# Keeping twelve instead of nine feed-forward blocks of an image for its successor's stage in a convolution-attention and feed-forward kernel

## The reference

```
x = x + conv(ln_over_channels(x))      # linear attention over 32 heads of dim 8
t = tokens(x)                          # 1024 tokens x 256
t = t + ffn(ln_over_channels(t))       # 6 experts of width 341, gated per image

conv: qkv = 1x1(x); agg = grouped 1x1(depthwise 5x5(qkv)); heads from [qkv, agg]
      kv = relu(k)^T [v, 1]; out = relu(q) kv; out = out[:8] / (out[8] + eps)
      then 1x1 projection and batch norm
ffn:  token_repr = mean over tokens; softmax over 11 router logits; top 2;
      expert weights from a fixed table; h = gelu(t W1 + b1);
      sum over experts of weight * (h W2 + b2)
```

## Time and profile before

| | |
|---|---|
| time, median of 3 runs | 1707.79 us (1707.75 to 1715.56) |
| the profiled execution: time | 1710.06 us |
| its span | 1708.3 us |
| PE busy (matmul) | 1370.4 us, 80% |
| DVE busy | 1281.9 us, 75% |
| ACT busy | 1059.6 us, 62% |
| POOL busy | 970.8 us, 57% |
| mean DMA rate | 19 GB/s |

### The profile page before, as it was taken

How to read it: one execution, slowest core, us unless ns; L and a number is a source line. 1 busy time by engine, 2 the same in 40 slices (tenths; PEclk the granted TensorE clock), 3 DMA queues, 4 the chain that set the end, 5 groups by cost and what they waited for, 6 DMA issues and landing times.

```text
span 1708.3 us, 18712 instructions
## 1 busy us (share of the span) xinstructions
PE 1370.4 (80%) x6844; PEld 786.2 (46%) x6844; DVE 1281.9 (75%) x1305; ACT 1059.6 (62%) x1855; POOL 970.8 (57%) x746
## 2 busy tenths in 40 slices
PE   5516557699878989699878989699878987999598
PEld 3215435455444545455444545355444444545343
DVE  3995999896959976896959966896959987880000
ACT  3444435577648765677648765677657865675376
POOL 3682726466558557465567556475565647344444
PEclk7758779899989999899989999899989999999899
DMA  5100000000001100100001100100001000100000
GB/s 174 74 25 1 25 1 1 0 26 13 1 0 38 37 1 1 38 25 13 1 1 38 38 1 1 38 1 13 1 1 37 13 1 1 37 13 1 13 1 25
DMA packets 14251, 32.75 MB, mean 19 GB/s; under 512 B 2384, under 2 KB 5328, under 8 KB 13904
## 3 DMA queue, kind: packets, MB, share of 16 engines
q1 hardware_dynamic: 14160, 31.56, 5.3%
HBM read 23.17 MB, written 8.39 MB: 18 GB/s over the span
## 4 chain that ended last, share of the span: by engine, by line
PE 48%; ACT 19%; POOL 13%; DVE 11%; issue 8%; DMA 1%; SPq 0%; POOLq 0%; ACTq 0%; DVEq 0%
PE wbk L542 20%; PE acc L555 12%; DVE dacc L1121 8%; PE wbk L634 7%; POOL dwo L939 4%; ACT gh L739 4%; ACT hb L740 3%; PE wbk L644 2%; PE wbk L593 2%; ACT tapb L714 2%; POOL tl L903 2%; POOL gl L969 2%; ACT sum_b L819 1%; ACT qkvs L790 1%; PE wbk L608 1%
## 5 line engine op out<-in xcount | busy, mean ns | idle before, releaser
L1121 DVE SCALAR_TENSOR_TENSOR dacc<-qkvs,dww,dacc 128x930 f32<-128x930 f32 (+4 forms) x954 | 1053.0, 1184 | 0.0
L969 POOL TENSOR_TENSOR gl<-hb,gh 128x512 f16<-128x512 f32 x256 | 303.5, 1187 | 385.3 <-ACT hb L740 384.6
L834 ACT ACTIVATE hb<-wbk,b1s 128x512 f32<-128x512 f32 x256 | 175.0, 684 | 201.2 <-PE wbk L542 201.0
L939 POOL TENSOR_TENSOR dwo<-dwo,tapb 128x992 f32<-128x992 f32 (+1 forms) x104 | 240.9, 2316 | 11.7 <-ACT tapb L714 8.4
L542 PE MATMUL wbk<-th,w1h 128*128 128x512 f16 x512 | 158.1, 391 | 104.7 <-POOL tl L903 65.4
L555 PE MATMUL acc<-gh,w2h 128*128 128x512 f16 x512 | 197.8, 386 | 13.6 <-POOL gl L969 13.5
L555 PE MATMUL acc<-gl,w2h 128*128 128x512 f16 x512 | 197.6, 386 | 0.0
L555 PE MATMUL acc<-gh,w2l 128*128 128x512 f16 x512 | 197.3, 385 | 0.0
L739 ACT ACTIVATE gh<-hb,ewg 128x512 f16<-128x512 f32 x256 | 182.3, 712 | 4.1 <-DVE ewg L1074 4.1
L740 ACT ACTIVATE hb<-hb,ewg 128x512 f32<-128x512 f32 x256 | 181.8, 710 | 0.0
L1025 DVE RECIPROCAL den<-den 128x128 f32<-128x128 f32 x32 | 30.4, 949 | 199.4 <-ACT den L813 199.4
(11 more groups left out here) (146 smaller groups left out, 2225.0 us busy)
## 6 DMA issues: line engine op xcount, KB each, us to landing
xa<-x SPq DMA_DIRECT2D x8, 1024.0 KB, 5.0
yr<-x SPq DMA_DIRECT2D x8, 1024.0 KB, 5.0
out<-yr SPq DMA_DIRECT2D x16, 512.0 KB, 2.8
dwo<-w SPq DMA_DIRECT2D x1, 2048.0 KB, 11.1
yr<-w SPq DMA_DIRECT2D x2, 1024.0 KB, 15.8
dwo<-w_qkv SPq DMA_DIRECT2D x1, 768.0 KB, 4.6
wp<-w_proj SPq DMA_DIRECT2D x1, 512.0 KB, 11.9
pw<-w_pw SPq DMA_DIRECT2D x16, 24.0 KB
```

The costliest lines, as they stand in the source:

```text
L834: last = nc.scalar.activation(hb[:, f % GB, :], b[:], ACT.Gelu, bias=b1s[:, f % FT:f % FT + 1], scale=1.0 / (X_SCALE * W_SCALE))
L939: ins = nc.gpsimd.tensor_tensor(d3[:, oy, ox], d3[:, oy, ox], t3[:, iy, ix], ALU.add)
L969: nc.gpsimd.tensor_tensor(gl[:, f % GB, :], hb[:, f % GB, :], gh[:, f % GB, :], ALU.subtract).then_inc(g_low, 1)
L1121: ins = nc.vector.scalar_tensor_tensor(out=dst[:, oy, ox], in0=i3[:, jy, jx], scalar=dww[:, m, tap:tap + 1], in1=a3[:, oy, ox], op0=ALU.mu ...
```

## The change

`KEEP` goes from 9 to 12; nothing else is changed. No instruction is added or removed.

```diff
-KEEP = 9
+KEEP = 12
```

## The result

The changed kernel takes **1687.66 us** (median of 4 runs, 1680.61 to 1688.38) where the kernel before, run beside it, takes 1711.41 (4 runs). The ratio is 0.9851, interval 0.9811 to 0.9892: some 25 us less, interval 18 to 32. Forecast were 46 less.

A forecast was written before the change was run, and what follows sets the result against it. TensorE and ScalarE in turn, plus TensorE's hole before `low`, set the period. Five periods of 3.57 + 2.8 (31.9 us) and 14.2 in the last images give 46.1 less: 1662 us, range 1648 to 1680.

The forecast's parts named there:

- What bounds the kernel: Whole period: no engine alone; TensorE and ScalarE one after the other, plus TensorE's 7.59 us hole before `low`.
- Part 1: Ahead of `agg`, iterations 1 to 5: ScalarE drains 5.65 us earlier, two moved taps cost 2.08; gain 3.57 per period.
- Part 2: Around `low`, iterations 2 to 6: two blocks moved into TensorE's hole gain 2.8 us per period, bounds 0 and 4.9.
- Part 2, order and times: Around `low`: a split delays `scale`, `low` ends 3.3 us later, and TensorE keeps a wait of 2.1 us.
- Part 2, the clock: Behind the shorter wait for `low`: full clock instead of 0.50 for 3.8 us, which cost 1.9 us.
- Part 2, behind the exponentials: Second half of `agg`: takes 2.0 us at full clock instead of 3.09, ending 2.8 earlier than before.
- the hole only moves: Rival around `low`: it gets later than 3.3 us or the half clock returns; 30.5 us gained, 1677 us; chance 0.16.
- Iteration 6: Before `agg` of half 1: three blocks go without taps, at TensorE's pace of 2.59 us each; gain 7.8 us.
- Iteration 7: First stage: VectorE becomes the bound, `agg` waits for it some 4 us and comes 7.2 us earlier.
- The tail: Behind the last `agg`: moved blocks make `rbc` 2.1 us late, `stats` regains 1.3 by clock; net 0.8 late.
- Slower: Rival at `agg`: GpSimd's mask, ready at 602.3 instead of 597.2, makes the gain there nothing; 1717 us; chance 0.05.
- The whole hole closed: Rival around `low`: no wait remains, clock stays up; 8.5 us per period, 56.7 in all, 1651 us; chance 0.14.

The follow-up runs named there:

- repeated run: The changed kernel itself measured once more, beside the kernel before on one chip: 1686.26 us, ratio 0.9854.
- the first experiment: Against the changed kernel, both `low` put before the moved blocks' ScalarE and GpSimd parts, TensorE's order the same: 1664.9 us, ratio 0.973.
- tail version: Against the first experiment, one block behind the last image's `rnorm` instead of two, another in its wait for `low`: 1658.5 us; with 28 useless matmuls there, 1659.51.

## Why the prediction was wrong in size

- **What bounds the kernel: right.** The chain keeps its shares, a block in the hole is a gain for the waits.
- **Part 1: right**, and its two terms too. ScalarE drains `agg` directly behind its tap (394.86); the moved tap (407.62) costs 1.0. Net 3.63 per image against 3.57. That nothing ate it, neither the mask nor VectorE's pair 0, shows in the same 4.64 for all five images in every kernel with this edit.
- **Part 2, order and times: right.** The remaining split ahead of `scale` (1.16 us), `scale` at 487.66, `low` ends at 493.8, 18.0 us after the reciprocal began, where the old place was 14.6: 3.4 later, forecast 3.3. The wait left is 2.16, forecast 2.1.
- **Part 2, the clock: wrong, and this is the failed step.** "I take full clock behind the new, shorter wait." The granted clock there is 0.50 for 5 us in three of five images and 0.66 and 0.70 in two. The row for it was at hand, with its price, and I read it as belonging to the length of the wait. Filling the wait in either kernel gives 1.7 to 2.7 us per image. The forecast's own times show that the 1.9 that `exp` was to come earlier was the clock alone: block 0 starts 3.2 us later (694.15 against 690.96), and 3.1 us of `back` and `logits` (695.40 to 698.52 in the kernel before) no longer stand behind it. As the lower clock stayed, for nearly as long as before, nothing was left. The Trainium skill (TensorE: Matmul & The Clock Gate, "Why this matters for your kernels") says that gaps between bursts of matmuls bring the lower clock back. The gaps that it names are longer than this one; here the trace shows it behind a wait of 2.16 us, in all five images, and the trace decides.
- **Part 2, behind the exponentials: not gained either, and mis-read.** The 3.09 us of the earlier trace rows for the second half of `agg` are those of one image. In the kernel before it took 2.05, 3.09, 2.05, 3.11 and 2.05 us, so the 0.9 was there to be gained in two images, not in five. In the changed kernel it took 2.66, 2.05, 2.05, 2.97 and 2.77. The stage to `fin` lost 0.6 us in all in one profile and 5.3 in the other, by the clock.
- **The rival that came closest.** The prediction priced a staying half clock at 1.9 a period, 9.5 in all (36.6 gained); together with what was missing behind the exponentials it took the whole 2.8. That is *the hole only moves* (part 2 gives nothing, 30.5 gained), by its second condition, the returning half clock; a `low` later than 3.3, its first, did not come (3.4 against 3.3). Measured are 25, less than even that, for the reasons below and the 1.1 lost around `low`.
- **Iteration 6: mis-sized, 4.5 instead of 7.8.** I priced the three blocks at TensorE's pace, as if the others could follow it. TensorE came early, stood 2.37 us for ScalarE and went on at a mean of 0.63; the last of the three blocks gave 0.11 here instead of 2.59. VectorE still waited 6.65 us before its step 16, so it was not in the way.
- **Iteration 7: nearly right, 5.9 instead of 7.2.** `agg` waits 4.09 us for VectorE's `dwo` (forecast 4); VectorE became the bound. But its eight matmuls took 5.21 us instead of 3.69, at a clock of 0.72 behind that wait: 1.5 us, the missing part. The repeated run shows 4.7 in this iteration.
- **The tail: right but for the last step.** `stats` and `rbc` begin with sixteen matmuls in 2.02 and 1.95 us, at full clock, as estimated. Lost 0.19 and 0.86 in the two runs up to the last but one event, against 0.8; the 1.68 at the end comes and goes.
- **The other rivals fell.** *Slower* needed the mask to hold `att`; part 1 excludes it. *The whole hole closed* (1651) is not what the change does; the first experiment does it, with 4.3 gained per image up to `exp` and 3.7 up to `fin`, against the 4.9 of that case.

**How far the cause goes, and what stays open.** The transposes are not needed for the lower clock: in iteration 6 of the changed kernel TensorE works without a gap up to 1335.7 (1333.82 + 1.88), waits 2.37 us, and the clock is down for 3.4 of the 4.6 us that follow; nor do they bring it without a wait, as the first experiment shows. Open is where the bound lies for a wait of about 2 us: the one of 1.95 behind the exponentials was followed by 0.66 in the changed kernel (508.20) and by 1.00 in the tail version (503.90), with the same order on TensorE but another wait before it. The two tail versions, with and without the 28 matmuls, are the same up to the tail, and in iteration 4 TensorE is at full clock in both for over 12 us up to this wait: behind it the clock is 1.00 for 5 us in one (872.8) and falls to the lower level 1.1 us on in the other (875.5). So neither the length of the wait nor the work before it decides by itself.

## What to carry to other kernels

In this kernel a wait costs its length and what the clock does behind it, and the second may be as much behind 2 us as behind 7.6. Shortening a wait buys its length only if the clock is read behind the new one, and until a trace shows it the old price stays in the sum; a handful of useless matmuls in the remaining wait is a cheap experiment that gives that price (12 us here, in either kernel). A clock row is read in every period before it is priced: one period showed 3.8 us at the lower level, three others over 5. When a block is moved into a hole of one engine, follow its parts through the other engines' queues: the same TensorE order with the split and the Gelu behind `low` gave 21 us more by the ratios. And a block taken away is worth no more than what the next late engine lets through: the third of iteration 6 was worth 0.11 us of its 2.59, and taking a fourth cost 2.3 in the next iteration, where it had filled a wait.

## What the runs showed of the hardware

- The granted clock was 0.50 for 2.8 to 5.9 us behind waits of 2.16 us, and 0.63 in the mean over 4.6 us behind one of 2.37 that followed gapless work. Behind waits of 1.04 and 0.28 us it was 1.00; behind 1.95 us it was 0.66 in one kernel and 1.00 in another. Behind waits of 7.59 us it was 0.50 for 3.7 to 5.5 us, so a wait of under a third of the length brought nearly as much of the lower clock.
- Filling a wait with matmuls gave 12.7 us in the kernel before and about 12 in the changed one, with all other work the same.
- The same kernel's start-up, up to the first `fin`, differs by up to 5 us between runs of kernels that don't differ there; the very end by 0 or 1.68 us, and the 1.68 goes with 3.4 us at the lower clock behind the last exponentials. Two profiles of the changed kernel itself differ by 4.7 us from `exp` to `fin`, over five images.
- With ScalarE's table load of 1.28 us and the exponentials ahead of the second pair of drains, TensorE stood 1.95 us in the middle of `agg`; with them behind the first pair of drains it did not, and a wait of 0.95 us was left behind `agg`.
